# Decoder layer with a mixture of experts: slots planned in two parts, and one transpose of the start moved

## The reference

```
x = layernorm(x + attention(x))                 # 16 heads of 16
x = layernorm(x + cross_attention(x, context))  # 16 heads of 16, 64 keys
logits = x @ router_w.T                         # 8 experts
probs  = softmax(logits); vals, idx = top_k(probs, 2)
for e in range(8):
    w = sum(where(idx == e, vals, 0))
    out = out + w[:, None] * (gelu(x @ w1[e].T) @ w2[e].T)   # 256 -> 1024 -> 256
x = layernorm(x + out)
```

## Time and profile before

| | |
|---|---|
| median of three runs | 845.76 us |
| profiled execution | 842.24 us, span 840.2 us |
| TensorE busy | 718.2 us (85%) |
| VectorE, ScalarE, GpSimd busy | 329.5, 287.2, 220.0 us |
| chain that ended last | TensorE 73%, VectorE 10%, ScalarE 5%, DMA 5%, issue 3%, GpSimd 2% |

### The profile page before, as it was taken

The page is one execution under the profiler, slowest core; times in us unless marked ns, Lnnn a source line. Parts: engine busy times, 40 slices in busy tenths (PEclk is TensorE's granted clock), DMA queues, the critical chain, the costliest instruction groups (busy, mean ns, idle before and its releaser), DMA issues.

```text
span 840.2 us, 11562 instructions
## 1 busy us (share of the span) xinstructions
PE 718.2 (85%) x3963; PEld 465.7 (55%) x3964; DVE 329.5 (39%) x742; ACT 287.2 (34%) x525; POOL 220.0 (26%) x278
## 2 busy tenths in 40 slices
PE   6899999999998678888979630799999999999970
PEld 3322333322224353647544520799999999999970
DVE  3687776788864360726444430000000000000004
ACT  2246656666764315251433220111111111111112
POOL 2201111111145201010140353133333333333322
PEclk9869999999999899998999655899999999999995
DMA  5974032434341400001030943466665656666506
GB/s 157 185 175 82 5 89 64 77 90 102 58 128 43 151 0 1 1 1 50 1 51 1 226 125 79 148 187 182 172 167 166 172 179 184 179 182 182 166 12 200
DMA packets 58908, 92.80 MB, mean 110 GB/s; under 512 B 13841, under 2 KB 45298, under 8 KB 57331
## 3 DMA queue, kind: packets, MB, share of 16 engines
q1 hardware_dynamic: 50355, 83.86, 36.4%
q0 software_dynamic: 8512, 8.44, 6.2%
HBM read 75.94 MB, written 17.86 MB: 112 GB/s over the span
## 4 chain that ended last, share of the span: by engine, by line
PE 73%; DVE 10%; ACT 5%; DMA 5%; issue 3%; POOL 2%; SPq 1%; POOLq 0%; DVEq 0%; ACTq 0%
PE ps L1705 17%; PE ps L1716 16%; PE ps L1432 7%; PE ps L1423 7%; PE ps L1357 6%; PE ps L1461 3%; DVE nmx L999 3%; PE ps L1375 2%; PE ps L1544 2%; POOL metas L740 2%; ACT probs L828 2%; PE ps L1582 1%; PE ps L1444 1%; PE ps L1572 1%; PE ps L1575 1%
## 5 line engine op out<-in xcount | busy, mean ns | idle before, releaser
L828 ACT ACTIVATE probs<-ps 128x512 f32<-128x512 f32 x256 | 136.0, 603 | 102.7 <-PE ps L1423 102.0
L999 DVE TENSOR_REDUCE nmx<-ps 128x1 f32<-128x512 f32 x256 | 159.8, 681 | 15.7 <-PE ps L1357 15.2
L1705 PEld LDWEIGHTS ps<-xtT,w1c 128*128 128x128 f32 x1248 | 147.3, 194 | 4.3 <-issue 2.4
L1705 PE MATMUL ps<-xtT,w1c 128*128 128x128 f32 x1248 | 147.7, 277 | 1.8 <-ACT xtT L952 1.8
L1716 PE MATMUL ps<-wexp,hidT 128*128 x624 | 141.0, 379 | 0.0
L1319 DVE TENSOR_SCALAR yw<-ps,mt 128x256 f32<-128x256 f32 x39 | 18.9, 484 | 290.5 <-PE ps L1716 290.5
L1716 PEld LDWEIGHTS ps<-wexp,hidT 128*128 128x128 f32 x624 | 115.6, 190 | 14.2
L958 ACT ACTIVATE hidT<-ps 128x1024 f32<-128x1024 f32 x39 | 40.0, 1024 | 229.9 <-PE ps L1705 229.9
L781 POOL DMA_INDIRECT acc<-yw,mt x39 | 61.9, 1587 | 171.9 <-DVE yw L1319 171.9
L1357 PE MATMUL ps<-kst,qst 96*128 96x512 bf16 x256 | 99.2, 409 | 4.9 <-DVE nmx L999 3.3
L1423 PE MATMUL ps<-qst,kst 99*128 99x512 bf16 x256 | 93.9, 390 | 1.1 <-ACT probs L828 0.7
(11 more groups left out here) (192 smaller groups left out, 773.1 us busy)
## 6 DMA issues: line engine op xcount, KB each, us to landing
w1c<-in_w1T SPq DMA_DIRECT2D x39, 1024.0 KB, 5.6
wexp<-in_w2T SPq DMA_DIRECT2D x8, 1024.0 KB, 9.7
kst<-scrk SPq DMA_DIRECT2D x48, 128.0 KB, 7.0
qst<-scrq SPq DMA_DIRECT2D x8, 384.0 KB, 4.8
xTb<-in_xT SPq DMA_DIRECT2D x4, 512.0 KB, 7.6
qst<-scrq SPq DMA_DIRECT2D x8, 256.0 KB, 5.4
xr<-in_x SPq DMA_DIRECT2D x4, 512.0 KB, 5.2
x2d<-xr SPq DMA_DIRECT2D x4, 512.0 KB, 6.0
```

Source lines behind the costliest of these rows:

```text
L828: act.activation(probs[n % 8][:, :], ps[:, 4 + n % 3, :], ACT.Exp).then_inc(s_exp, 1)
L999: dve.tensor_reduce(nmx[w % 2][:, k:k + 1], ps[:, ring_bank("max", w, k), :], AX.X, ALU.max, negate=True).then_inc(s_mfree, 1)
L1705: mm = pe.matmul(ps[:, 2 * (j % 2) + f // 4, f % 4 * P:(f % 4 + 1) * P], w1c[j % 2][:, k * FF + f * P:k * FF + (f + 1) * P], xtT[j % 2][:, ...
```

## The change

**Two plans.** After three batches 3072 pairs are placed. An expert with c pairs has floor(c/128) full blocks, so that at least 24 - 7 = 17 blocks are full (`EARLY`), whatever the routing. `plan_early` runs in stage 5 on VectorE, behind the routing of batch 2 and behind the residual sum of tile 1 of batch 3; it fills slots 0 to 16 with full blocks. `plan_rest` runs behind the routing of batch 3 and gives the other 22 slots. In stage 5 `slots(2)` comes ahead of `norm_o(1, 3, 3)`, and on TensorE `positions` ahead of `end_step(…, 3)`.

**Who waits for what.** SyncE loads metas and w1 for slot 0 after the first plan and the scatters of batches 0 to 2. It now issues the w2 loads 3 to 6 in one go behind the store of batch 2; the store of batch 3 comes behind w1 of slot 1. The groups of metas are now (0), (1 to 3), (4 to 7), (8 to 11), (12 to 16), and so on. On GpSimd `scatter_metas(2)` stands ahead of `rstd_of(1, 3)`; then come gathers 0 and 1, `scatter_metas(3)`, gather 2, and the loop. On TensorE: the logits of batch 3, turn 0, hidden 0, `positions(3)`, turn 1, hidden 1, the second count, turn 2, expert_out 0, and the loop, which is now two loops (slots 4 to 15, then 16 to 35). The routing of batches 2 and 3 uses PSUM bank 7 and not 1. Some buffers have traded places in SBUF.

**The start.** The turned maxima of unit 0 stand behind the third maximum of unit 1 (`FIRST_TURN_AT = 2`) and not behind the eighth.

The core of the diff:

```diff
-META_GROUPS = tuple((t, min(t + 4, NSLOT)) for t in range(0, NSLOT, 4))
+EARLY = 2 * (NB - 1) * S // P - NE + 1
+META_GROUPS = ((0, 1), (1, 4), (4, 8), (8, 12), (12, EARLY), (EARLY, 20), (20, 24), (24, 28), (28, 32), (32, 36), (36, NSLOT))
...
-            if k == TURN_AT and w > 0:
+            if w > 0 and k == (FIRST_TURN_AT if w == 1 else TURN_AT):
                 order.append(("turn", w - 1))
...
         load_expert(2)
-        load_expert(3)
         store_x2(2)
-        load_expert(4)
-        load_expert(5)
-        store_x2(3)
-        sp.wait_ge(s_lg, NB)
-        load_expert(6)
-        sp.wait_ge(s_pos, NB)
-        sp.wait_ge(s_x2[0], 16 * NB)
-        sp.wait_ge(s_x2[1], 16 * NB)
+        for e in range(3, 7):
+            load_expert(e)
...
+        sp.wait_ge(s_on, NE_TILES)
         sp.wait_ge(s_planned, 1)
-        load_w1(0, 0)
-        for i in range(2):
-            sp.wait_ge(s_disp[i], 16 * NT)
+        sp.wait_ge(s_disp[0], 16 * 2 * QT * 2)
+        sp.wait_ge(s_disp[1], 16 * 2 * QT)
...
         load_metas(0)
+        load_w1(0, 0)
+        load_metas(1)
         load_w1(1, 1)
-        load_metas(1)
+        load_metas(2)
+        store_x2(NB - 1)
...
+                if lo == EARLY and t == EARLY - 5:
+                    sp.wait_ge(s_planned, 2)
+                    sp.wait_ge(s_disp[1], 16 * 2 * QT * 2)
+                if group > 2 and lo - 5 == t:
+                    load_metas(group)
...
-        for t in range(3):
+        for t in range(2):
             gather(t)
+        scatter_metas(NB - 1)
+        gather(2)
         for t in range(NSLOT):
+            if t + 3 == EARLY:
+                for k in range(2):
+                    pool.wait_ge(s_x2l[k], 16)
...
+        def plan_early():
+
+            dve.wait_ge(s_cnt, 1)
+            plan_step(dve.tensor_copy(cnt[:, :], ps[0:1, 6, 0:NE]))
+            plan_step(dve.tensor_tensor(w3, cnt[:, :].unsqueeze(2).to_broadcast([1, NE, CAP]),
+                                        steps1[:, :].unsqueeze(1).to_broadcast([1, NE, CAP]), ALU.is_ge))
+            plan_step(dve.tensor_reduce(ntile[:, :], w3, AX.X, ALU.add))
+            tiles_before(ntile[:, :])
+            plan_step(dve.tensor_scalar(spare[:, :], ntile[:, :], -1.0, float(CAP), ALU.mult, ALU.add))
+            slot_plan(0, EARLY, 0.0)
+            plan_step(dve.tensor_tensor(room[:, :], ntile[:, :], ends[:, :], ALU.subtract))
+            plan_step(dve.tensor_scalar(room[:, :], room[:, :], float(EARLY), 0.0, ALU.add, ALU.max))
+            plan_step(dve.tensor_tensor(done_early[:, 0:NE], room[:, :], ntile[:, :], ALU.min))
...
+            if r is not None:
+                slots(r)
+            if e2 is not None:
                 norm_o(1, e2, 3)
                 add_residual(1, e2, 1)
-            if r is not None:
-                slots(r)
+            if r == NB - 2:
+                plan_early()
             if e2 is not None:
                 add_residual(1, e2, 2)
                 add_residual(1, e2, 3)
...
         pe.wait_ge(s_planned, 1)
-        pe.wait_ge(s_we, 16 * NE)
...
         turn_tile(0, 0, 0)
         hidden(0, 0, 0)
+        positions(NB - 1)
         turn_tile(1, 1, 0)
-        for j in range(4):
+        hidden(1, 1, 0)
+        count(NB - 1, 7, 128)
+        turn_tile(2, 0, 1)
+        pe.wait_ge(s_we, 16 * NE)
+        expert_out(0, 0)
+        for j in range(1, 4):
             tile(j, j, 0)
-        with pe.Fori(1, NSLOT // 4) as i:
+        with pe.Fori(1, EARLY // 4) as i:
+            for j in range(4):
+                tile(4 * i + j, j, i)
+        pe.wait_ge(s_planned, 2)
+        with pe.Fori(EARLY // 4, NSLOT // 4) as i:
             for j in range(4):
                 tile(4 * i + j, j, i)
```

More of the change, by code:

```diff
@@ L220, in decoder_layer @@
     q2t = at_expert(3, "q2t", KD * S, F32)
-    qh = [sb("qh0", KD * S, F32R, R_K)]
-    ql = [sb("ql0", KD * S, F32R, R_K)]
+    qh = [at_expert(6, "qh0", KD * S, F32R)]
+    ql = [at_expert(6, "ql0", KD * S, F32R)]
+    ybuf2 = [sb(f"ybuf2_{i}", D, F32, R_K) for i in range(QT)]
+    xTs2 = sb("xTs2", KD * S, F32, R_K)
     assert place[R_K] <= LATE
@@ L409, in tiles_of, with router_bank @@
         return QT * E_AT[ph, b]
-    RB, RC = 1, 0
+    def router_bank(b):
+        return 1 if b < NB - 2 else 7
     def ring2(i):
@@ L680, in _ @@
             fill(pool.affine_select(out=v, in_=v, compare_op=op, fill=0.0, base=0, pattern=pattern, channel_multiplier=cm))
-        for m, step, n, start in ((first_row, T, NE, 0), (steps, P, CAP, 0), (numbers, 1, NSLOT, 0), (falling, -1, NE, NE)):
+        for m, step, n, start in ((first_row, T, NE, 0), (steps, P, CAP, 0), (numbers, 1, NSLOT, 0), (falling, -1, NE, NE), (steps1, P, CAP, P)):
             fill(pool.iota(m[:, :], [[step, n]], base=start, channel_multiplier=0, allow_small_or_imprecise_dtypes=True))
+        fill(pool.memset(done_early[:, :], 0.0))
         for k in range(2):
@@ L748, in _, with known, checked @@
                 add_bias(n)
-            if 0 <= n - 2 < NB:
+            if 0 <= n - 2 < NB - 1:
                 rstd_of(1, n - 2)
[L751 to L755, removed]
+            if 0 <= n - 3 < NB - 1:
                 scatter_metas(n - 3)
+            if n == NB + 1:
+                rstd_of(1, NB - 1)
+                break
         nothing, last_row = pool.alloc_register("nothing"), pool.alloc_register("last_row")
         pool.reg_mov(nothing, 0)
-        def checked():
-            pool.reg_add(last_row, nothing, T - 1)
+        def known(t):
+            return (NB - 1) * S if t < EARLY else T
+        def checked(t):
+            pool.reg_add(last_row, nothing, known(t) - 1)
             return dict(bounds_check=last_row, oob_is_err=False)
@@ L1221, in _, with plan_step, tiles_before @@
         dve.wait_ge(s_fill, FILLED)
+        planned = [0]
+        def plan_step(ins):
+            planned[0] += 1
+            ins.then_inc(s_plan, 1)
+            dve.wait_ge(s_plan, planned[0])
+        w3 = wide[:, 0:NE * CAP].rearrange("p (e j) -> p e j", j=CAP)
+        w2 = wide[:, 0:NE * NE].rearrange("p (e j) -> p e j", j=NE)
+        def tiles_before(tiles):
+            plan_step(dve.tensor_tensor(w2, upto[:, :].rearrange("p (e j) -> p e j", j=NE),
+                                        tiles.unsqueeze(1).to_broadcast([1, NE, NE]), ALU.mult))
+            plan_step(dve.tensor_reduce(ends[:, :], w2, AX.X, ALU.add))
@@ new lines, in slot_plan @@
+        def slot_plan(lo, hi, skipped):
+            n = hi - lo
+            wt = wide[:, 0:n * NE].rearrange("p (t e) -> p t e", e=NE)
+            wt2 = wide2[:, 0:n * NE].rearrange("p (t e) -> p t e", e=NE)
+            tne = [1, n, NE]
+            plan_step(dve.tensor_tensor(wt, numbers[:, 0:n].unsqueeze(2).to_broadcast(tne),
+                                        ends[:, :].unsqueeze(1).to_broadcast(tne), ALU.is_ge))
+            plan_step(dve.tensor_reduce(planf[0][:, 0:n], wt, AX.X, ALU.add))
+            plan_step(dve.tensor_scalar(planf[0][:, 0:n], planf[0][:, 0:n], float(NE - 1), None, ALU.min))
+            plan_step(dve.tensor_copy(plan[0][:, lo:hi], planf[0][:, 0:n]))
+            plan_step(dve.tensor_tensor(wt2, wt, spare[:, :].unsqueeze(1).to_broadcast(tne), ALU.mult))
+            plan_step(dve.tensor_reduce(planf[1][:, 0:n], wt2, AX.X, ALU.add))
+            plan_step(dve.scalar_tensor_tensor(out=planf[1][:, 0:n], in0=planf[1][:, 0:n], scalar=skipped,
+                                               in1=numbers[:, 0:n], op0=ALU.add, op1=ALU.add))
+            plan_step(dve.tensor_scalar(planf[2][:, 0:n], planf[1][:, 0:n], float(PAD_BLOCK), float(P), ALU.min, ALU.mult))
+            dve.tensor_copy(plan[1][:, lo:hi], planf[2][:, 0:n]).then_inc(s_planned, 1)
@@ L1279, in _ @@
             stage(n)
[L1282 to L1312, removed]
+        plan_rest()
         def weigh(t):
@@ L1414, in _ @@
                 next_half(w, k)
-                if k == TURN_AT and w > 0:
+                if w > 0 and k == FIRST_TURN_AT:
                     max_turn(w - 1)
@@ L1669, in stage @@
                 pv2(x, 1)
+            if r == NB - 2:
+                count(r, 6, 0)
             e2_step(4)
@@ L1681, in stage, with count @@
                 pv2(x, 3)
-        for n in range(NB + 3):
+        def count(b, at, col):
+            pe.wait_ge(s_rt, RT * (b + 1))
+            pe.matmul(ps[:, at, col:col + NE], onesb[:, :], base[:, :], start=True, stop=True).then_inc(s_cnt, 1)
+        for n in range(NB + 2):
             stage(n)
-        pe.wait_ge(s_rt, RT * NB)
-        pe.matmul(ps[:, RB, RC + 128:RC + 128 + NE], onesb[:, :], base[:, :], start=True, stop=True).then_inc(s_cnt, 1)
+        for pair in range(2):
+            turn_x(1, NB - 1, pair)
+        logits(NB - 1, range(QT))
         def turn_tile(t, j, turn):
```

67 lines of the change are left out of this document (45 added, 22 removed).

## The result

The changed kernel takes 836.32 us, the median of four runs (834.2 to 839.62), against 846.56 us (845.61 to 849.11) for the kernel before in the same comparison; the ratio is 0.9878, with a 95% interval of 0.9835 to 0.9921. The forecast was 834.7 us with a range of 830.8 to 840.5, and a gain of 11.1 us; the medians differ by 10.2. Run again later it took 837.49 us (eight runs, 836.16 to 845.16) against 846.61, ratio 0.9907 (0.9874 to 0.994). The profiled execution took 835.05 us, span 833.3, against 842.24 and 840.2: 6.9 us less. That pair has less between it than the medians have, because the profiled execution of before was quicker than all the other runs of its kernel.

What follows compares the result with a forecast made beforehand. TensorE's hole before the first expert_out, a wait ending on the last scatter of metas, was taken as the bound. Moving that start from 540.02 to 528.9 saves 11.1 us: 845.76 - 11.1 = 834.7 us, range 830.8 to 840.5.

Steps and rivals of the forecast that it cites:

- the slack of ScalarE: Before hidden 0: ScalarE is free at 502.7, 2.1 us ahead of hidden 0 at 504.8.
- the landing of gather 2: GpSimd, behind batch 3's scatters: gather 2 is issued at 522.1 and lands 3.95 us later, bounds 3.2 to 4.4.
- the clock: TensorE falls to half clock in the wait for tile 2, costing expert_out 0 2.0 us, bounds 0 and 3.5.
- `slot` 1.7 us sooner: Routing of batch 2 in stage 5: moving slots(2) and positions forward has slot written 1.7 us sooner, about 480.3.
- The landing of the scatters: Batch 2's last scatter, issued at 489.5, lands 6.57 us later, bounds 4.3 and 11.2; metas are read from 496.1.
- Rival (a): Unfinished w2 loads make batch 2's scatters land after 11.2 us: gain 6.5, 839.3 us; chance 0.18.
- The plan hidden: VectorE's first plan is ready before 487.5, ahead of the scatters' landing; the residual sums end about 5 us later, 490.2.
- What is late next: GpSimd's batch 3 scatters, from 511.9, delay gather 2 to 522.1; TensorE waits ten microseconds at tile 2, expert_out 0 at 526.9.
- The start, the loop, the tail: Earlier first turn taken as 0, loop 0 with 7.25 us per tile (entry 0 to 0.5), tail unchanged.
- (b): Cheap end: scatters land in 4.3 us and the clock doesn't fall, gain 15.2, 830.6 us; chance 0.10.
- (c): No TensorE wait at tile 2: expert_out 0 follows hidden 1 at about 516, gain 24 us, 821.8; chance 0.02.
- (d): Slower: SyncE's queue of w2 and x loads starves slot 0; at 120 GB/s the time is 852; chance 0.04.

Runs made afterwards that it cites:

- experiment 5: The changed kernel with the first plan moved behind the residual sums of tiles 2 and 3 of batch 3 on VectorE: 842.60 us, one execution.
- experiment 8: The changed kernel with gathers a tile further ahead, batch 3's scatters handed out in the loop, and the first plan behind batch 3's residual sums: 822.60 us.
- experiment 1: The changed kernel with gather 2 ahead of the eight scatters of batch 3 on GpSimd: 827.03 us, ratio 0.9797.
- experiment 3: The changed kernel with the first turn back behind the eighth maximum, the start's change undone: 838.29 us, ratio 0.9903.
- experiment 2: The changed kernel with gather 2 first and the eight scatters of batch 3 handed out in GpSimd's loop: 823.42 us, ratio 0.972.
- both fillers: The changed kernel with 96 or 32 identity matmuls behind the second count, in TensorE's wait for tile 2: 851.23 us and 836.95 us.
- the short one: The changed kernel with 32 identity matmuls in TensorE's wait for tile 2: 836.95 us, ratio 0.9887.

## Why the prediction was right, step by step

The mechanism was the right one at each step but one (the slack of ScalarE); the sum was right to a microsecond by the medians (11.1 foretold, 10.2 measured, 9.1 in the repeat), and four microseconds too large by the two profiles, where two terms were mis-sized: the landing of gather 2 by 2.9 us and the clock by 1.0. The terms came from a profile and can only be judged by profiles, so that the medians agree to a microsecond is in part luck. The range doesn't need that luck: a gain of 7 us is inside it too.

- **`slot` 1.7 us sooner.** Right: from the routing's first step of batch 2 to the start of the step that writes `slot` it takes 9.4 us in place of 10.9, 1.5 less. But that first step came 1.17 us later than in the before (472.00 against 470.83), where the prediction had taken everything ahead of stage 5 as unchanged, so `slot` is there at 481.6 and not at 480.3, and the last scatter of batch 2 is issued at 490.74 and not at 489.5.
- **The landing of the scatters.** I took 6.57 us between 4.3 and 11.2. The changed kernel shows 5.06; the repeat and experiments 5 and 8 show 4.56, 4.06 and 6.75. Rival (a), full queues, is out. The 2.0 us that the Trainium skill (DMA: Bandwidth & Descriptors, Anatomy of one DMA) gives as the fixed cost of such a DMA is not borne out by a scatter here: the shortest of the before took 3.0 us, and this one 5.06.
- **The plan hidden.** Wrong in size. VectorE's sums ended with `nm` at 492.66, 7.3 us after the before's, not 5. Of this 1.17 us were there at the first step of the routing, and the out projection of tile 3 took 2.04 us where it had taken 1.10: TensorE had stood for five microseconds, and the granted clock was 0.50 from 488 to 490, a term that I left out. So `nm` came after GpSimd was free, and ScalarE was free at 504.7, where 502.7 was foretold. The slack of 2.1 us that the prediction gave ScalarE was gone: its table and gather 0 were ready together. The turn of tile 0 ended at 504.62 and its copy began at 504.65:

```profile
503.96 0.66 PE L1751 MATMUL ps<-identf,xt 128*128 128x128 f32 x2 [1.46 <-DMA xt<-x2d,mt]
```

```profile
504.65 0.38 ACT L972 ACTIVATE xtT<-ps 128x256 f32<-128x256 f32 x1
```

  So in this execution the late sums cost next to nothing. In the repeat the copy stood 0.4 us behind the end of the turn, in experiments 1 and 3 1.2, where gather 0 was sooner. Hidden 0 at 505.18, foretold 504.8, is right because misses cancel: the last scatter was issued 1.2 us later than foretold, landed 1.5 us quicker, and from there to hidden 0 it took 9.4 us and not 8.7. The timeline of VectorE:

```profile
488.44 0.15 DVE L1287 TENSOR_TENSOR done_early<-room,ntile 1x8 f32<-1x8 f32 x1
488.63 0.42 DVE L1119 TENSOR_TENSOR ybuf<-ps,xr 128x256 f32<-128x256 f32 x1
...
491.28 0.42 DVE L1119 TENSOR_TENSOR ybuf<-ps,xr 128x256 f32<-128x256 f32 x1 [1.55 <-PE ps L1510]
```

- **What is late next.** Right, and the main point. First scatter of batch 3 at 511.66 (foretold 511.9), gather 2 at 522.15 (522.1). Its landing is the term that was mis-sized: 6.85 us against 3.95. The rows of gathers that I took it from had nothing just ahead of them on their queue; this one had eight scatters. The trace of the before could have said so: the 35 gathers behind a scatter of outputs bring the median of all to 5.1 and the maximum to 6.2 (experiment 1). The upper bound should have been that, or the scatters' own 6.57, and not 4.4. From the landing to `expert_out 0` it took 1.0 us and not 0.8.
- **The clock.** Half clock behind the wait, as said; 3.0 us against 2.0. The price of a cold start was 2.0 in hidden 0 of the before, and in `expert_out 0` it was 3.0 by the chain; by the timelines, where a steady one is 3.62, it was 2.8, in the repeat 2.3 (5.95) and in experiment 3 1.5 (5.14): it varies with when the clock rises (0.89 of full from 534 to 536 in experiment 3, 0.61 in the changed kernel, 0.50 in its repeat). Windows of the changed kernel:

```profile
522.00:524.00 2.00, 0.00 (x0) 0.00 (x0) 0.00 (x0) 0.00 (x0) 1.54 (x2) 0.50 0.60 192
...
534.00:536.00 2.00, 2.00 (x7) 1.65 (x6) 0.00 (x0) 0.00 (x0) 0.00 (x0) 0.61 0.00 0
536.00:538.00 2.00, 2.00 (x19) 1.95 (x18) 0.48 (x1) 0.00 (x0) 0.14 (x1) 1.00 0.00 0
```

- **The start, the loop, the tail.** Taken at 0, and 0.1, 0 and 0 were measured; the second loop and the groups of metas cost nothing that the traces show, and the period of a tile is 7.25 us as before.
- **The other rivals.** (b) needed a landing of 4.3 us and a clock that stays; it was 5.06, and the clock fell. (c) could not be with the order as it stood; experiment 2 shows that it was an order away: 823.42 us against 836.32. (d) did not come: the w2 loads were through by about 491.

Left open: why the profiled pair shows 6.9 us and the medians 10.2. The intervals of both comparisons hold 7 us as well. Counted from the routing's first step of batch 2, the pair differs by 8.1 us (369.4 against 361.3), and the repeat by 7.5. The spread in the start and in the cross-attention is large enough for the rest, as the table of stretches shows; whether the moved `slots` and `positions` of stages 3 and 4 have a part in it was not tried.

## What to carry to other kernels

A change that brings one engine's work forward is worth no more than the next thing queued ahead of what that engine then needs: follow the order on every queue until the loop has its full pace, not to its first instruction. Work that is only needed later, here eight small scatters of 1.28 us each, belongs in the slack of the loop, not ahead of a gather that the loop waits for; moving them, with the gathers one tile further ahead, was worth 15 us (821.19 against 836.32; ratios to the before 0.9691 and 0.9878), more than the change itself. A time to landing is read from rows that have the same things ahead of them on their queue. And when a gain is small against the spread, compare stretches between fixed events, not totals.

## What was not expected of the hardware

- A gather of rows issued right behind eight scatters of 8-byte entries took 6.3 to 8.0 us to its turn in six executions. The first four of the before, with no scatter just ahead, took 3.2 to 4.4 to land, and the slowest of all its 39 took 6.2.
- TensorE's stream had gaps that no semaphore explains while scatters of metas were in flight: in experiment 1 hidden 2 was broken by pauses of 1.03, 0.45 and 0.45 us, and both fillers by several of 0.46 and 1.05 us, as in this timeline of the short one:

```profile
523.23 0.27 PE L1796 MATMUL ps<-identf 128*128 128x128 f32 x1 [0.46 <-issue]
...
525.39 0.59 PE L1796 MATMUL ps<-identf 128*128 128x128 f32 x2 [1.06 <-issue]
```

  What the engine waited for was not tried. In eight of the eleven changed executions one matmul of stage 4, at 437.40 in the changed kernel, comes after 1.56 to 1.74 us of idle time, where it was 0.18 in the before; the trace puts this down to VectorE's maxima, and whether it is of the same kind is not shown.
- The stretch from unit 0 to unit 15 is the same to 0.2 us in all twelve executions, while the stretch in which the clock rises, in the first microseconds of scores, moves by up to 2.9 us.
